# A Macaron transformer on one core: the FFN walks its blocks in pairs, the routers make slots before they normalise

## The reference

```python
x = x + 0.5 * ffn0(norm(x))     # silu(x w1[e]) * (x w3[e]), then w2[e]; hidden 256
x = x + attn0(norm(x))          # causal, window of 32
x = x + 0.5 * ffn0(norm(x))
x = x + 0.5 * ffn1(norm(x))     # gelu(x W1[e] + b1[e]), then W2[e] + b2[e]; hidden 512
x = x + attn1(norm(x))          # full attention inside the layer, with its own norm and residual
x = x + 0.5 * ffn1(norm(x))

# routing, both layers: logits = x @ router; top 2; softmax over the two (layer 0)
# or over all eight and renormalised (layer 1); out = sum over the two of weight * expert(x)
```

## Time and profile before

| | kernel before |
|---|---|
| median of 3 runs | 3512.67 us |
| profiled execution, its own time | 3517.73 us |
| span of the profile | 3516.0 us, mean granted TensorE clock 0.916 |
| TensorE busy (matmuls) | 2689.5 us, 76% |
| VectorE busy | 1769.7 us, 50% |
| GpSimd busy | 1635.7 us, 47% |
| ScalarE busy | 1451.2 us, 41% |
| routers(0) | about 20 to 262 us |
| ffn(0) | about 270 to 513 us |
| ffn(1) | about 1284 to 1531 us |
| routers(2) | about 1537 to 1800 us |
| ffn(2) | about 1802 to 2085 us |
| ffn(3) | about 3168 to 3450 us |

### The profile page before, as it was taken

How to read it: one execution, slowest core, us unless ns; L and a number is a source line. 1 busy time by engine, 2 the same in 40 slices (tenths; PEclk the granted TensorE clock), 3 DMA queues, 4 the chain that set the end, 5 groups by cost and what they waited for, 6 DMA issues and landing times.

```text
span 3516.0 us, 70275 instructions
## 1 busy us (share of the span) xinstructions
PE 2689.5 (76%) x22942; PEld 1669.6 (47%) x22942; DVE 1769.7 (50%) x5530; ACT 1451.2 (41%) x3050; POOL 1635.7 (47%) x1868
## 2 busy tenths in 40 slices
PE   2218977999999958842259979999999999959992
PEld 1216654666666636632247852333333333327781
DVE  3433325555555533345522227888788888832224
ACT  0103323444444423310124434666666666634441
POOL 4664553555554345545544454253443533134441
PEclk9999997999999979975579987999999999979996
DMA  6112222222221123222222222111111111012225
GB/s 148 39 49 77 79 76 76 65 64 65 64 67 52 34 81 102 77 74 70 60 67 68 68 63 64 35 45 46 36 53 37 48 35 35 21 30 69 68 69 156
DMA packets 264270, 222.57 MB, mean 63 GB/s; under 512 B 66278, under 2 KB 244460, under 8 KB 263404
## 3 DMA queue, kind: packets, MB, share of 16 engines
q1 hardware_dynamic: 229372, 146.98, 15.3%
q0 software_dynamic: 34560, 71.11, 6.1%
HBM read 114.00 MB, written 107.53 MB: 63 GB/s over the span
## 4 chain that ended last, share of the span: by engine, by line
PE 57%; issue 10%; another core or an unknown queue 7%; DVE 7%; POOL 7%; DMA 5%; ACT 5%; SPq 2%; ACTq 0%; POOLq 0%; DVEq 0%
PE PS L498 10%; PE PS L589 9%; PE PS L502 7%; PE PS L678 7%; POOL slot_inputs L1062 6%; PE PS L626 6%; PE PS L647 5%; DMA slot_inputs<-xs,slots 3%; PE PS L697 3%; ACT arena L827 3%; PE PS L630 2%; DVE mxs L1380 2%; PE PS L634 2%; PE PS L655 1%
## 5 line engine op out<-in xcount | busy, mean ns | idle before, releaser
L1062 POOL DMA_INDIRECT slot_inputs<-xs,slots x512 | 505.7, 988 | 1001.6 <-DVE slots L1246 573.7
L921 ACT ACTIVATE arena<-PS 128x512 f32<-128x512 f32 (+1 forms) x1344 | 699.7, 586 | 401.6 <-PE PS L647 186.1
L1069 POOL DMA_INDIRECT choice_outputs<-arena x568 | 546.4, 962 | 565.0 <-DVE arena L1352 254.3
L1380 DVE TENSOR_REDUCE mxs<-PS 128x1 f32<-128x512 f32 x1024 | 651.3, 683 | 176.4 <-PE PS L626 171.0
L827 ACT ACTIVATE arena<-PS 128x256 f32<-128x256 f32 (+2 forms) x586 | 253.8, 445 | 443.4 <-PE PS L502 158.6
L626 PE MATMUL PS<-w,q 96*128 96x512 f16 x1024 | 396.5, 389 | 30.3 <-DVE mxs L1380 27.4
L647 PE MATMUL PS<-q,w 100*128 100x512 f16 x1024 | 388.1, 382 | 17.1 <-ACT arena L921 16.9
L1383 DVE TENSOR_REDUCE mxs<-PS 128x2 f32<-128x320 f32 x512 | 247.2, 489 | 287.0 <-PE PS L634 173.9
L1337 DVE TENSOR_TENSOR arena<-PS,arena 128x256 f16<-128x256 f32 x284 | 119.9, 422 | 515.7 <-ACT arena L827 441.4
L589 PE MATMUL PS<-W,arena 128*128 x2272 | 293.2, 281 | 10.9 <-issue 6.8
L502 PE MATMUL PS<-ident,arena 128*128 128x128 f32 x1084 | 199.9, 286 | 124.2 <-DMA arena<-slot_inputs 104.3
(11 more groups left out here) (178 smaller groups left out, 3999.0 us busy)
## 6 DMA issues: line engine op xcount, KB each, us to landing
arena<-slot_inputs SPq DMA_DIRECT2D x284, 129.0 KB
G<-choice_outputs SPq DMA_DIRECT2D x128, 256.0 KB
qk_parts<-qk SPq DMA_DIRECT2D x64, 256.0 KB, 2.1
q<-qk_parts SPq DMA_DIRECT2D x128, 96.0 KB
choice_outputs<-arena POOLq DMA_INDIRECT x568
slot_inputs<-xs,slots POOLq DMA_INDIRECT x512
qk_parts<-qk SPq DMA_DIRECT2D x64, 128.0 KB, 2.0
W<-qk_parts SPq DMA_DIRECT2D x128, 48.0 KB
```

The source lines that it names most:

```text
L921: activate(pT[:, u % PTR, 0:n], PS[:, SC0 + u % NSC[a], 0:n], ACT.Exp, scale=SCALE).then_inc(s_pe, 1)
L1062: g.indirect_dma_start(Xs, bass.IndirectOffsetOnAxis(ap=slots[:, s, c, k:k + 1], axis=0), xs[:, n % XSR, k], None).then_inc(s_scat[c][n % ...
L1069: g.indirect_dma_start(Yt, bass.IndirectOffsetOnAxis(ap=xid[:, b % XRING, j, D:D + 1], axis=0), yb[:, b % YRING, j], None).then_inc(s_ysc[ ...
L1380: vec.tensor_reduce(mxs[:, m % 2, p % NT, QROWS + col:QROWS + col + 1], PS[:, MX0 + u % NMX], AX, ALU.max)\
```

## The change

- FFN, all engines: the loop takes blocks b and b+1 together. TensorE: up b, up b+1, turn b+2, turn b+3, down b-2, down b-1. ScalarE: activated b, turned b+2, turned b+3, activated b+1, the staged weights, stored b-2, stored b-1. VectorE: gated b, turned b+2, turned b+3, gated b+1, register loads of both, the staged weights, stored b-2, stored b-1.
- Buffers: activations four (HRING) in place of two, results eight (YRING) in place of four, normalised router rows four (XSR) in place of three. The arena grows from 8704 to 8720 columns.
- `routers` of VectorE: `router_slots` of i-1 stands before `router_norm` of i, not after it.

```diff
-YRING = 4
-XSR = 3
+YRING = 8
+HRING = 4
+XSR = 4
...
@@ TensorE, ffn
-                expert(0)
-                expert(1)
-                turned(0)
-                for b in range(NBLK + LAG):
-                    if b + 2 < NBLK:
-                        expert(b + 2)
-                    if b + 1 < NBLK:
-                        turned(b + 1)
-                    if b < NBLK:
-                        up(b)
-                    if b >= LAG:
-                        down(b - LAG)
+                for b in range(2):
+                    expert(b)
+                    turned(b)
+                for b in range(0, NBLK + 3, 2):
+                    two = (b, b + 1)
+                    for n in two:
+                        if n + 2 < NBLK:
+                            expert(n + 2)
+                    for n in two:
+                        if n < NBLK:
+                            up(n)
+                    for n in two:
+                        if n + 2 < NBLK:
+                            turned(n + 2)
+                    for n in two:
+                        if 0 <= n - 2 < NBLK:
+                            down(n - 2)
@@ ScalarE, ffn
-                    if b >= 2:
-                        eng.wait_ge(s_y, blk(f, b - 2))
+                    if b >= HRING:
+                        eng.wait_ge(s_y, blk(f, b - HRING))
...
+                for b in range(0, NBLK + 3, 2):
+                    two = (b, b + 1)
+                    if b < NBLK:
+                        activated(b)
+                    for n in two:
+                        if n + 2 < NBLK:
+                            turned(n + 2)
+                    if b + 1 < NBLK:
+                        activated(b + 1)
+                    for n in two:
+                        if f >= 2 and n + 2 < NBLK:
+                            expert(n + 2)
+                        staged(n)
+                    for n in two:
+                        if f < 2 and 0 <= n - 2 < NBLK:
+                            stored(n - 2)
@@ VectorE, routers
                         router_diff(f, i - 1)
+                        router_slots(f, i - 1, 4 + (i - 1) % 2)
                     if valid(i):
                         router_norm(f, i)
                     if valid(i - 1):
-                        router_slots(f, i - 1, 4 + (i - 1) % 2)
                         router_weights(f, i - 1)
@@ VectorE, ffn
+                turned(0)
+                turned(1)
+                for b in range(0, NBLK + 3, 2):
+                    two = (b, b + 1)
+                    if f < 2 and b < NBLK:
+                        gated(b)
+                    for n in two:
+                        if n + 2 < NBLK:
+                            turned(n + 2)
+                    if f < 2 and b + 1 < NBLK:
+                        gated(b + 1)
+                    for n in two:
+                        if f >= 2 and n < NBLK:
+                            expert(n)
+                        staged(n)
+                    for n in two:
+                        if f >= 2 and 0 <= n - 2 < NBLK:
+                            stored(n - 2)
```

More of the change, by code:

```diff
@@ L39 @@
 HID = [2, 2, 4, 4]
-LAG = 1
 LITTLE = 15
 XRING = 8
-YRING = 4
-XSR = 3
+YRING = 8
+HRING = 4
+XSR = 4
 AHEAD = 8
@@ L871, in activated @@
                     if f < 2:
[L872 to L874 removed]
+                        if b >= HRING:
+                            eng.wait_ge(s_gt, blk(f, b - HRING))
+                        activate(hact[:, b % HRING, 0:2 * BS], u[:, 0:2 * BS], ACT.Silu, scale=1 / WS).then_inc(s_act, 1)
                         return
[L876 to L877 removed]
+                    if b >= HRING:
+                        eng.wait_ge(s_y, blk(f, b - HRING))
                     for c in range(C):
[L879 removed]
+                        ins = activate(hact[:, b % HRING, c * BS:(c + 1) * BS], u[:, c * BS:(c + 1) * BS],
                                        ACT.Gelu_apprx_tanh, bias=b1c[:, bass.ds(off[b] + c, 1)], scale=1 / WS)
@@ L893, in stored, with staged @@
                     copy(flat(yb[:, b % YRING]), PS[:, YB + b % 2, 0:BS]).then_inc(s_yev, 1)
-                turned(0)
-                if f >= 2:
-                    expert(0)
-                for b in range(NBLK + LAG + 1):
-                    if b + 1 < NBLK:
-                        turned(b + 1)
-                    if b < NBLK:
-                        if f >= 2 and b + 1 < NBLK:
-                            expert(b + 1)
-                        activated(b)
-                    if f < 2 and b >= LAG + 1:
-                        stored(b - LAG - 1)
+                def staged(b):
                     if f == 1 and b >= 2 and second_at(b - 2) is not None:
@@ L910, in ffn @@
                         copy(second[k][1][:, 0], restage[:, k % 2], WS).then_inc(s_rhs, 1)
+                for b in range(2):
+                    turned(b)
+                    if f >= 2:
+                        expert(b)
+                for b in range(0, NBLK + 3, 2):
[14 more added lines that the diff above has]
+                            stored(n - 2)
             def attention(a):
@@ L1353, in stored, with staged @@
                                       bcast(b2b[:, bass.ds(off[b], D)], BJ, 1), ALU.add).then_inc(s_yev, 1)
-                turned(0)
-                for b in range(NBLK + LAG + 1):
-                    if b + 1 < NBLK:
-                        turned(b + 1)
-                    if f < 2 and b < NBLK:
-                        gated(b)
-                    if f >= 2 and b < NBLK:
-                        expert(b)
-                    if f >= 2 and b >= LAG + 1:
-                        stored(b - LAG - 1)
+                def staged(b):
                     if f == 1 and b >= 3 and second_at(b - 3) is not None:
```

18 lines of the change are left out of this document (7 added, 11 removed).

## The result

| | before | after |
|---|---|---|
| median of the runs beside each other (4 and 4) | 3512.60 us | 3465.82 us |
| lowest to highest | 3510.0 to 3515.03 | 3456.39 to 3466.82 |
| profiled execution, span | 3517.73, 3516.0 | 3456.39, 3454.6 |

The ratio is 0.9861 (95%: 0.9842 to 0.988): 1.4% faster, where the prediction had 3523 us and slower as the likelier side. 3465.8 lies inside the range.

The account below looks back on a forecast made before the run. The FFNs were taken as bound by the loop scatter, release, store, with scatter bursts holding TensorE's signals. +42 + 8 - 15 - 28 = +7, plus 3 for staged copies, gave +10 on 3512.7: 3523 us, range 3440 to 3570.

Parts of the forecast that it names:

- The hold as the bound: Both layers' FFNs: bursts of four scatters hold TensorE's signals until 1.0 to 1.2 us after their end, bounding the loop.
- This lies between 1.9 (let through) and 3.5 (held), nearer to the held one; I take held.: First layer's FFNs: turns ending 2.8 and 3.0 us into the burst were taken to be held until after it.
- the loop of 7.5 us: First layer's FFNs: scatter, release and store in the pair walk take 7.5 us a pair, against 6.93 before.
- First layer: +42 forecast: First layer's two FFNs under the pair walk: 263 us each against 242, +21 us twice.
- Second layer, +8: Second layer's FFNs: held and passing loops alternate, 8.0 us a pair against 7.89, +4 us per FFN.
- the limit of 7.9 to 8.3: Second layer's FFNs: TensorE's 7.24 us a pair plus what it loses by running only twenty products ahead.
- Staged copies, +3: FFNs: 3 us added for staged weight copies in ScalarE's path and the breaks they cause.
- Routers, -15 and -28: Router stages: slots made earlier start scatters 1.1 us sooner 14 times in the first layer, 1.9 us 15 times in the second.
- Edits at nothing: Eight result buffers, four activation buffers, block loads and the larger arena were costed at nothing; the loads had 2 us left.
- (a): Rival, FFNs: turns pass before the hold begins; loop 6.5 us, -14 per first-layer FFN, total 3450 us; chance 0.22.
- (b): Rival, routers: no gain, because the positions' signal waits as long as the landing did; total 3563 us; chance 0.12.
- (c): Rival: scatters hold nothing and TensorE becomes the bound everywhere, -139 us, total 3374 us; chance 0.08.

Follow-up runs that it names:

- e3: The changed kernel with only the first of each FFN block's two scatters, result buffer cleared at the start, half the result rows left out: 3402.68 us in one run.
- e4: A separate program, not the kernel: TensorE steps answered by ScalarE beside GpSimd scatters, clears or plain DMAs; greatest lag 1.12 us with 4 scatters, 5.59 with 8.
- e16: A separate program like e4, with longer stretches and no VectorE copies ahead of the bursts, on a chip with the hold: greatest lag 6.82 us with 8 scatters.
- e2: The changed kernel with ScalarE's staged weight copies moved behind the pair's stores: 3453.39 us, ratio 0.9833.
- e15: e2's kernel where GpSimd's odd-block scatters also wait for the next pair's first first-product, on a chip with the hold: 3446.25 us, ratio 0.982.
- e1: The kernel before with the change's buffers and router order, but the old FFN walk one block at a time: 3471.86 us, ratio 0.9888.
- e14: The same program as e16, unchanged, on a chip without the hold: at most 0.07 us of lag in the sections named for it.

## Why the prediction was wrong, point by point

- *The hold as the bound.* Right, and shown: e3 takes the long bursts away and e4 isolates them, and on chips without the hold the four FFNs of before are 84 us shorter. The chips differ by 206.6 us of 3516; the prediction looked for the hold in FFNs and routers only, and most of the rest is in the attentions.
- *"This lies between 1.9 (let through) and 3.5 (held), nearer to the held one; I take held."* **This is the step that failed**, and with it the loop of 7.5 us. The geometry was nearly right (turns forecast to end 2.8 and 3.0 us into the burst, measured 2.97 and 3.19 into that of 266.87) and so was the price (7.56 measured). What was wrong is the choice between the two ends: in all 30 bursts of ffn(0) where the first turn ended at most 2.97 us into them it got through. I had read the hold as a gate that shuts at one time, from two rows, and it is a slow delivery: in e16 single releases get through every 0.7 to 2.1 us of a held stretch. One turn that was copied at 4.34 us into the burst let TensorE begin the next pair at 272.39, before the release, and from 274.08 on its turns end early enough in the burst to be copied inside it (2.59 and 3.57 us into that of 326.15). The forecast loop ran once, a half-held one of 7.21 us followed, and then loops of 6.5 for nearly the whole stage. First layer: +42 forecast, -6.2 measured.
- *Second layer, +8.* The alternation was forecast and is there, but with a mean of 7.7 and 7.6 us a pair and not 8.0: -9.7 and -11.5 us in place of +4 each. The two loops came out nearly as worked out (8.2 to 8.7 for 8.3 to 8.7, and 6.7 to 6.9 for 6.7); what was too high is the limit of 7.9 to 8.3 that TensorE was to set.
- *Staged copies, +3.* ffn(1) came out 10.6 us above ffn(0)'s difference (+2.2 against -8.4), with four bursts of eight that no term had. With the staged copies behind the stores (e2) it is 3.5 us shorter and the bursts stay; in e15, where only one of six is left, it is 10.7 us shorter.
- *Routers, -15 and -28.* -23.3 and -16.9 by stage, -40.2 in sum. Bursts 12.46 and 13.57 us apart against 12.2 and 13.6 forecast. The sum is nearly right, by two errors that cancel. In routers(0) only seven of the fifteen steps of before are the 13.3 to 13.4 us that I multiplied. The first four are longer, 66.8 us in sum, and 59.8 in after; all fifteen give 17.0 us, the start of the first burst 0.8, and 5.5 come behind the start of the last burst. Why these parts fell is open. In routers(2) I had multiplied one of the longest steps, 15.55 us; ten of before run from 14.9 to 15.6, the other five from 11.7 to 14.1. e1, without the walk, has -20.1 and -18.5.
- *Edits at nothing.* e1 bears this out for the buffers: eight result and four activation buffers moved no FFN stage of the old walk by over 2.1 us. The block loads were close to their limit, as said: a turn waited 1.58 and 1.23 us for one, and each time a loop of 7.5 us followed.
- *Rivals.* (a) was right in mechanism for ffn(0): 6.53 against its 6.5 us. It gave -14 per FFN, measured were -8.4 and +2.2, and 3450 us for the total against 3465.8. It had a chance of 0.22. (b) is refuted. (c), no hold at all, is refuted here, and is how three other chips are. There a pair takes 6.2 us and not the 6.02 of (c), in the old walk too, so the walk in pairs gains nothing without a hold.
- *The rule on engines.* The Trainium skill says in "Trainium Architecture — The Big Picture", section "What this means for kernel authors", that an engine doesn't block another without a semaphore between them. In both micro runs no semaphore stands between GpSimd's scatters and the engines that run beside them. The rule agrees with e14 (0.05 us of lag beside 8 scatters) and not with e16 (6.82).

## What to carry to other kernels

When a release comes late behind another engine's work, read several loops before you treat it as a gate: a slow delivery lets single signals through, and then the loop can slip out of the slow rhythm that its first round shows. Work out both rhythms and ask which one holds itself up, rather than which one the first loop falls into. Here an order that puts the turns early into a burst, and leaves behind it only the signal that the next burst waits for, hid a part of the hold, and changed the FFNs by 1.4 us where there was none. And before you work on a time that the profile puts down to no one, see whether another chip of the kind has it: here 200 of 3512 us were gone on other chips.

## What the runs showed of the hardware

- Chips differ: the kernel before took 3511 and 3511 us on two of the chips that experiments fell on, 3311, 3312 and 3312 on three. The lag beside indirect DMAs is there on the first two and absent on the three, and single instructions last the same. Why these chips have it stays open; no run here separates the chip from what else may have gone on beside it.
- Where it is, 4 scatters issued in a row make signals up to 1.12 us late, 8 make them 6.82 late (5.59 in e4), 8 half-sized ones 7.44, 4 gathers 2.43. Beside 4 clears, 4 plain DMAs of GpSimd and 4 DMAs of SyncE the lag is 0.05 us at most.
- In a held stretch the late releases come in steps of 0.72 us (e16, from 34.43 to 43.02), and this holds for ScalarE's answers and TensorE's starts alike.
- Beside products of 512 columns there was no lag (0.04 us), beside steps of three products of 256 columns 1.12: so what TensorE issues has a part in it; which, these runs don't tell.
- In e4 a scatter issued at 62.09 while VectorE copied f32 to f32 without a pause (40 copies, 60.87 to 66.38) took 5.11 us instead of 0.96, until 0.82 us behind the last copy.
